# Gate and up products of two of the four shared-expert batches as three fp32r products of parts, in an attention and mixture-of-experts kernel

## The chip, the cores and the metric

The kernel runs on one core of one Trainium2 chip. The metric is the device time of one execution in microseconds (us); lower is better. The core has a matrix engine (TensorE, PE in the profile), a vector engine (VectorE, DVE), an activation engine (ScalarE, ACT), a general engine (GpSimd, POOL) and a queue that only issues transfers (SyncE, SP). All of them read and write the on-chip memory SBUF; PE writes its sums to PSUM, which DVE and ACT read. The engines run by themselves and meet only in semaphores.

## The reference

One transformer block on 4 batches of 512 rows, width 256: a cross attention with 16 heads, then a mixture of 8 experts (2 per row) with a shared expert that every row passes. The change touches the shared expert:

```python
x = x + _L0_xattn_ref(_layernorm(x, axis=-1), ctx_1024, ctx_1024, ...)
x = x + _L0_ffn_ref(_layernorm(x, axis=-1), ...)
# in _L0_ffn_ref, xf is 2048 x 256, HALF = 384
logits = xf @ gate_w.T                      # routing: the two best of 8 experts
for e in range(E):
    g = xf @ wg[e].T
    u = xf @ wu[e].T
    y = jax.nn.silu(g) * u @ w_down[e].T
    out = out + comb[:, e:e + 1] * y
shared = jax.nn.silu(xf @ sg_gate.T) * (xf @ sg_up.T) @ sg_down.T
return (shared + out).reshape(b, t, d)
```

## The kernel before

Each engine has one program, in the order in which its code is written; there is no scheduler. The attention takes the first 262 us. The stretch from there to 318 us does four things at once:

- **Routing**, mainly on DVE: logits, the two best experts of each row, ranks within each expert, and one-hot matrices (`hot_slots`) that PE multiplies into the lists of rows per expert (L957, signal `hot_full`). DVE then writes `token_of` and signals `lists_ready`.
- **The shared expert**, by batch `b` (512 rows) and third `m` of its 384 hidden columns. `shared_up(b)` on PE makes a block of gate and up for each `m`: 4 fp32 matmuls of 128x128 by 512 columns (L910; each is two records in the profile). ACT takes the silu of the gate (`shared_silu`, L1209), DVE multiplies by up (`shared_h`, L1462), and when the three are there, PE multiplies by the down weights (`shared_down`, L920) and DVE adds the result to the rows (`shared_y`, L1484). The blocks alternate between two halves of PSUM, so block n waits for `shared_h` of block n-2.
- **The experts' up weights in two parts.** PE multiplies fp32 numbers in several passes. The kernel avoids it for the experts: a number is the sum of a high part, rounded to the format fp32r, and a low part, the remainder, and a product is the sum of high by high, high by low and low by high. The up weights come in 8 pieces of 128x1536: ACT rounds a piece (`hi_parts`, L1054 into `wup_hi`), DVE subtracts (`lo_part`, L1562 into `wup_lo`). Attention does the same for its projections (L723 to L725).
- **The first tiles of rows.** POOL fetches the rows of the expert tiles by their numbers in `token_of` (L615, indirect transfers, here called gathers). PE transposes a tile (`rows_t`, L969), ACT rounds it, and DVE subtracts (`rows_lo`, L1589), which frees the PSUM bank for the next tile.

Behind `shared_down(2)` PE turns to the experts (L982 to L984). They need all 8 low pieces and take 39 tiles to 475 us. The shared batch 3 and the sums of the experts close the program.

Batches 0, 1 and 2 are the ones before the experts. The change calls batches 1 and 2 "second" and "third". The normalised rows of each batch are stored to DRAM for the gathers (L460 on SP, the last batch at L1213 from ACT).

Of the kernel before, what the change touches and what calls it, by code (L numbers as in the profile page):

```python
# [41 lines left out]
DMA = 16  # L42


def build(nc, x, ctxT, wqT, bq, wkT, bk, wvT, bv, woT, bo, gwT, wupT, wdnT, sgT, suT, sdT, out):
    B, S, D = x.shape
# [5 lines left out]
    C = D // P  # L52
# [27 lines left out]
    with ExitStack() as ctx:  # L80
        def sb(name, shape, dt=F32):
            return ctx.enter_context(nc.sbuf_tensor(name, shape, dt))

        def sem(name):
            return ctx.enter_context(nc.semaphore(name))
# [48 lines left out]
        with nc.sbuf_tensor("e_hT_hi", [P, 2, M, P], F32R) as e_hT_hi, \  # L134
                nc.sbuf_tensor("e_hT_lo", [P, 2, M, P], F32R) as e_hT_lo:
            pass
        moe = sb("moe", [P, MOE])
        e_xT_hi = sb("e_xT_hi", [P, 2, C, P], F32R)
# [74 lines left out]
        lgT = sg[:, M - 1, :]  # L213
        TE = T * E
# [10 lines left out]
        def te():  # L225
# [30 lines left out]
        ld_k, ld_q, ld_ctx, ld_v, ld_o, ld_cv, ld_moe, ld_up = (sem(n) for n in  # L256
            ("ld_k", "ld_q", "ld_ctx", "ld_v", "ld_o", "ld_cv", "ld_moe", "ld_up"))
# [25 lines left out]
        s_up, s_sg, s_h, s_y, s_yfree = (sem(n) for n in ("s_up", "s_sg", "s_h", "s_y", "s_yfree"))  # L283

# [77 lines left out]
        EARLY = 4  # L362

# [10 lines left out]
        def _(sp):  # L374
# [80 lines left out]
            def rows_of(dram, b):  # L455
                return dram[b * S:(b + 1) * S, 0:D].rearrange("(k p) d -> p k d", p=P)

            for b in range(B - 1):
                sp.wait_ge(xs_ready, B + b + 1)
                sp.dma_start(rows_of(xn_d, b), xn2[:, b * QT:(b + 1) * QT, :]).then_inc(xn_stored, DMA)  # L460
# [3 lines left out]
            for c in range(C):  # L464
                sp.dma_start(wup[:, c, :], wupT[c * P:(c + 1) * P]).then_inc(ld_up, DMA)
# [11 lines left out]
        def _(pool):  # L477
# [129 lines left out]

            pool.wait_ge(pad_rows, DMA)
            pool.wait_ge(acc_zeroed, 2 * DMA)
            pool.wait_ge(xn_stored, DMA * B)  # L610
# [27 lines left out]
        def _(pe):  # L638
# [313 lines left out]
            shared_up(1)  # L952
# [8 lines left out]
            shared_up(2, 0, 2)  # L961
# [47 lines left out]
            shared_up(2, 2, 3)  # L1009
# [43 lines left out]
        def _(act):  # L1053
# [144 lines left out]
            def logits_copy(i, cols, src):  # L1198
                act.wait_ge(lt_full, i + 1)
                copy(lgT[:, cols], src).then_inc(lt_read, 1)  # L1200

            ln2_copies(2)
            logits_copy(0, slice(0, S - P), pv_bank[:, 0:S - P])
# [17 lines left out]
            def hi_parts(pieces):  # L1221
                for i in pieces:
                    copy(piece(wup_hi, i), piece(wup, i)).then_inc(up_hi, 1)
# [3 lines left out]
            act.wait_ge(ld_up, DMA * C)  # L1227
            hi_parts(range(0, EARLY))
            for m in range(M):
                shared_silu(1, m)  # L1230
            act.wait_ge(lists_ready, 1)
            act.wait_ge(who_stored, DMA)
            hi_parts(range(EARLY, EARLY + 1))
            shared_silu(2, 0)
            hi_parts(range(EARLY + 1, EARLY + 2))
            shared_silu(2, 1)
            hi_parts(range(EARLY + 2, SPLITS))
# [15 lines left out]
            shared_silu(2, 2)  # L1253
# [33 lines left out]
        def _(dve):  # L1287
# [175 lines left out]

            shared_h(0, 0)
            steps = [0]
# [94 lines left out]
            def lo_part(i):  # L1560
                dve.wait_ge(up_hi, i + 1)
                v.tensor_tensor(piece(wup_lo, i), piece(wup, i), piece(wup_hi, i), ALU.subtract).then_inc(up_lo, 1)  # L1562

            hot_slots(range(0, T))
            shared_y(0)
            hot_slots(range(T, T + T // 2))
            shared_h(1, 0)
            hot_slots(range(T + T // 2, NJ)).then_inc(hot_built, 1)
            shared_h(1, 1)
            lo_part(0)  # L1570
            shared_h(1, 2)
            lo_part(1)
# [5 lines left out]
            v.tensor_scalar(token_of[:], tok, io_np, None, ALU.add).then_inc(lists_ready, 1)  # L1578
            shared_y(1)

            lo_part(2)
            shared_h(2, 0)
            lo_part(3)
            lo_part(EARLY)
            shared_h(2, 1)
# [39 lines left out]
            shared_h(2, 2)  # L1625
            rows_lo(1, 1)
            lo_part(EARLY + 3)
# [91 lines left out]
```

## Time and profile before

| | |
|---|---|
| median of 3 runs | 492.02 us (491.89 to 492.53) |
| the profiled execution | 493.5 us, of it 491.8 us from the first instruction to the last (the span) |
| granted TensorE clock | 0.992 on average |
| busy in the span: PE, DVE, ACT, POOL | 453.9, 314.3, 218.7, 212.6 us |
| start of the experts on PE (L982) | 318.3 us, after the last block of `shared_down(2)` |

In the timeline a matmul's record runs on while the next has started, so the distance of two starts is the time that one costs. "Idle" in brackets is the time that the engine waited before a row, and for whom. Times are from the first instruction. L numbers are lines of the kernel before.

### The profile page before, as it was taken

To read this page: it belongs to the slowest core of one execution; us is meant where nothing else is said; L and a number is where in the kernel's file an instruction comes from. 1 tells how busy PE (TensorE), PEld (TensorE's weight loads), DVE (VectorE), ACT (ScalarE), POOL (GpSimd) and SP (SyncE) were. 2 spreads that over 40 slices of the span, in tenths; PEclk is the share of its full clock that TensorE was granted. 3 is DMA by queue.
4 is the path that set the end of the run, shared out by engine and by line. 5 is a ranking of instruction groups with operands and counts; after the bars stand their busy time and mean duration, and the time that the engine had idled before them with its cause. 6 is when DMAs were issued, how large, how long until landed. Compare 5 with 4: busy or idle time off the path is not lost.

```text
span 491.8 us, 10348 instructions
## 1 busy us (share of the span) xinstructions
PE 453.9 (92%) x3257; PEld 325.3 (66%) x3258; DVE 314.3 (64%) x651; ACT 218.7 (44%) x429; POOL 212.6 (43%) x212
## 2 busy tenths in 40 slices
PE   7879999899999999999978999999999999999993
PEld 5565353664447544564555546699999999999852
DVE  4975767667672856647975895955455545554446
ACT  2257776626573466656863343332232223223210
POOL 4105676743541237302622003036676666665420
PEclk9989999999999999999999999999999999999998
DMA  8592421412224121310398901014444444444379
GB/s 259 106 227 95 130 80 62 155 58 74 69 75 160 34 96 41 117 60 2 104 377 322 327 0 43 1 38 71 74 66 65 74 76 64 66 72 68 36 205 337
DMA packets 45580, 53.93 MB, mean 110 GB/s; under 512 B 7760, under 2 KB 41872, under 8 KB 44912
## 3 DMA queue, kind: packets, MB, share of 16 engines
q1 hardware_dynamic: 34320, 39.77, 25.2%
q0 software_dynamic: 7488, 10.31, 13.1%
q10 hardware_dynamic: 3744, 3.47, 2.7%
q8 instruction: 17, 0.28, 0.2%
q14 instruction: 11, 0.09, 0.1%
HBM read 27.09 MB, written 13.67 MB: 83 GB/s over the span
## 4 chain that ended last, share of the span: by engine, by line
PE 63%; DVE 18%; ACT 6%; DMA 5%; issue 4%; SPq 1%; DVEq 0%; ACTq 0%; POOLq 0%
PE set_a L659 7%; PE set_a L983 6%; PE set_a L984 6%; PE set_a L982 6%; PE set_b L689 6%; DVE attention L1379 4%; ACT attention L1133 4%; PE set_b L679 3%; PE set_b L1001 3%; PE set_a L890 3%; PE set_b L1002 3%; PE set_b L1003 3%; PE set_b L992 2%; PE set_a L701 2%; PE set_a L910 2%
## 5 line engine op out<-in xcount | busy, mean ns | idle before, releaser
L1379 DVE TENSOR_REDUCE attention<-set_a 128x2 f32<-128x1024 f32 (+2 forms) x96 | 95.9, 1040 | 26.4 <-PE set_a L661 24.4
L1133 ACT ACTIVATE attention<-set_b 128x512 f32<-128x512 f32 (+1 forms) x176 | 87.9, 569 | 49.4 <-PE set_b L679 36.1
L543 POOL TENSOR_SCALAR_AFFINE_SELECT attention<-attention 128x512 f32<-128x512 f32 x64 | 42.8, 683 | 89.7 <-ACT attention L1133 89.7
L623 POOL DMA_INDIRECT sum_rows<-moe,token_of x39 | 61.8, 1586 | 43.8 <-issue 29.5
L659 PE MATMUL set_a<-attention 96*128 96x512 bf16 (+3 forms) x256 | 61.5, 305 | 5.1 <-DVE attention L1379 4.8
L615 POOL DMA_INDIRECT e_x<-normed_rows,token_of x39 | 39.5, 1013 | 61.3 <-DVE token_of L1578 34.9
L1246 ACT ACTIVATE moe<-set_a 128x384 f32<-128x384 f32 x39 | 19.2, 492 | 105.0 <-PE set_a L984 105.0
L679 PE MATMUL set_b<-attention 99*128 99x512 bf16 (+3 forms) x256 | 58.9, 303 | 7.0 <-ACT attention L1133 5.3
L1603 DVE TENSOR_TENSOR moe<-set_a,moe 128x384 f32<-128x384 f32 x39 | 21.7, 558 | 62.8 <-ACT moe L1246 34.5
L659 PEld LDWEIGHTS set_a<-attention 96*128 96x128 bf16 x256 | 25.4, 99 | 44.9 <-DVE attention L1379 17.4
L982 PE MATMUL set_a<-wup_hi,e_xT_hi 128*128 x156 | 53.1, 340 | 0.0
L983 PE MATMUL set_a<-wup_lo,e_xT_hi 128*128 x156 | 52.9, 339 | 0.0
L984 PE MATMUL set_a<-wup_hi,e_xT_lo 128*128 x156 | 52.8, 338 | 0.0
L661 PE MATMUL set_a<-maskb,identb 128*128 128x128 bf16 x256 | 49.6, 222 | 0.0
L689 PE MATMUL set_b<-attention 128*32 128x128 f32 (+3 forms) x512 | 43.8, 441 | 1.3 <-POOL attention L543 1.2
L1001 PE MATMUL set_b<-w_down_hi,e_hT_hi 128*128 x117 | 36.4, 311 | 1.3 <-DVE moe L1615 0.8
L679 PEld LDWEIGHTS set_b<-attention 99*128 99x128 bf16 x256 | 19.2, 97 | 27.5 <-ACT attention L1133 18.2
L1054 ACT ACTIVATE attention<-set_b 12x512 bf16<-12x512 f32 (+4 forms) x48 | 26.0, 595 | 20.3 <-PE set_b L647 11.2
L524 POOL TENSOR_TENSOR attention<-attention 128x512 f32<-128x512 f32 x14 | 15.9, 1157 | 42.8 <-ACT attention L1054 21.4
L1003 PE MATMUL set_b<-w_down_hi,e_hT_lo 128*128 x117 | 32.9, 281 | 0.0
L1002 PE MATMUL set_b<-w_down_lo,e_hT_hi 128*128 x117 | 32.8, 281 | 0.0
L1054 ACT ACTIVATE attention<-attention 128x512 bf16<-128x512 f32 x32 | 19.2, 643 | 26.7 <-DVE attention L1327 21.2
(179 smaller groups left out, 893.7 us busy)
## 6 DMA issues: line engine op xcount, KB each, us to landing
attention<-attention SPq DMA_DIRECT2D x182, 64.0 KB, 2.6
wup<-in_wupT SPq DMA_DIRECT2D x2, 3072.0 KB, 14.6
sum_rows<-attention SPq DMA_DIRECT2D x2, 2048.0 KB, 13.5
wup<-sum_rows SPq DMA_DIRECT2D x8, 512.0 KB, 6.9
attention<-in_ctxT SPq DMA_DIRECT2D x7, 512.0 KB, 6.5
w_down<-in_wdnT SPq DMA_DIRECT2D x3, 1024.0 KB, 5.1
x_res<-in_x SPq DMA_DIRECT2D x4, 512.0 KB, 7.5
out<-x_res ACTq DMA_DIRECT2D x8, 256.0 KB, 4.0
```

Of the source, the lines that this page charges most:

```text
L623: g.indirect_dma_start(acc[i], bass.IndirectOffsetOnAxis(token_of[:, t:t + 1], 0), e_y[:, t % 2, :], None, compute_op=ALU.add).then_inc(ad ...
L659: mm(dst, qstack[0:ROWS, g // 2, h, k * P:w], kstack[0:ROWS, g // 2, h, 0:w], start=True, stop=False)
L661: last = mm(dst[:, k * P:w], identb[:], maskb[:], start=False, stop=True)
L679: last = mm(bank(par)[:, i * w:(i + 1) * w], kstack[0:ROWS + 3, g // 2, h, k * P:(k + 1) * P], qstack[0:ROWS + 3, g // 2, h, k * P:S], sta ...
L689: last = mm(pv_bank[32 * h:32 * h + 32, k * P:S], vaug[:, k, HG * g + h, :], pT[k][:, h, :], start=k == 0, stop=k == QT - 1, tile_position ...
L982: mm(dst, e_xT_hi[:, a, c, :], wup_hi[:, c, cols], start=c == 0, stop=False)
L983: mm(dst, e_xT_hi[:, a, c, :], wup_lo[:, c, cols], start=False, stop=False)
L984: last = mm(dst, e_xT_lo[:, a, c, :], wup_hi[:, c, cols], start=False, stop=c == C - 1)
L1001: mm(dst, e_hT_hi[:, a, m, :], wdn_hi[:, m, cols], start=m == 0, stop=False)
L1003: last = mm(dst, e_hT_lo[:, a, m, :], wdn_hi[:, m, cols], start=False, stop=m == M - 1)
L1133: nc.scalar.activation(pT[k][:, h:h + heads, :], bank(par)[:, 0:heads * (S - k * P)], ACT.Exp).then_inc(b_free, 1)
L1379: v.tensor_reduce(dst, src, AX.X, ALU.max, negate=True).then_inc(a_free, 1)
```

## The change

Batches 1 and 2 of the shared expert's gate and up are no longer made by fp32 matmuls but by `shared_up_parts`: 12 fp32r matmuls a block in place of 4 fp32 ones. For that ACT rounds the shared weights (2 copies of 128x768) and the rows of the two batches (2 of 128x1024), and DVE subtracts as often. The parts lie in the place of rows whose store to DRAM must be over first, so the store semaphore is split in three. `shared_up(2)` was cut in two with a `rows_t` between; now it is one piece. Pieces 0 and the last of the experts' weights get their low part on POOL (`up_low`), the other six on DVE. The high parts start when the first half of the weights has landed.

```diff
+        w_hi = moe_r[:, 0:2 * C * HALF].rearrange("p (a c n) -> p a c n", a=2, c=C)
+        w_lo = moe_r[:, 2 * C * HALF:4 * C * HALF].rearrange("p (a c n) -> p a c n", a=2, c=C)
+        x_hi = {1: second_hi[:], 2: moe_r[:, (B - 1) * QT * D:B * QT * D].rearrange("p (c n) -> p c n", c=C)}
...
+        PIECES = [0, 1, 2, 3, 6, 7, 4, 5]
...
+            def up_low(i):
+                pool.wait_ge(up_hi, i + 1)
+                w = PIECES[i]
+                g.tensor_tensor(piece(wup_lo, w), piece(wup, w), piece(wup_hi, w), ALU.subtract).then_inc(up_lo, 1)
+
+            pool.wait_ge(hot_built, 1)
+            up_low(0)
...
             for t in range(NX):
                 rows_in_tile(t)
+            up_low(SPLITS - 1)
...
+            def shared_up_parts(b, lo=0, hi=M):
+                pe.wait_ge(sw_lo, 2)
+                pe.wait_ge(sx_lo, b)
+                for m in range(lo, hi):
+                    n = b * M + m
+                    pe.wait_ge(s_h, n - 1)
+                    for a, dst in enumerate(gu[n % 2]):
+                        for c in range(C):
+                            high, low = w_hi[:, a, c, m * P:(m + 1) * P], w_lo[:, a, c, m * P:(m + 1) * P]
+                            mm(dst, high, x_hi[b][:, c, :], start=c == 0, stop=False)
+                            mm(dst, high, x_lo[b][:, c, :], start=False, stop=False)
+                            last = mm(dst, low, x_hi[b][:, c, :], start=False, stop=c == C - 1)
+                    last.then_inc(s_up, 1)
...
-            shared_up(1)
+            shared_up_parts(1)
...
-            shared_up(2, 0, 2)
+            shared_up_parts(2)
...
-            shared_up(2, 2, 3)
...
             ln2_copies(2)
+            act.wait_ge(xn_first, DMA * 2)
+            act.wait_ge(ld_moe, DMA * 4)
+            copy(w_hi[:, 1], wsu[:]).then_inc(sw_hi, 1)
+            copy(w_hi[:, 0], wsg[:]).then_inc(sw_hi, 1)
+            rows_hi(1)
...
             shared_h(0, 0)
+            dve.wait_ge(sw_hi, 2)
+            dve.wait_ge(xn_third, DMA)
+            for a, w in enumerate((wsg, wsu)):
+                v.tensor_tensor(w_lo[:, a], w[:], w_hi[:, a], ALU.subtract).then_inc(sw_lo, 1)
+            rows_low(1)
```

On DVE, from the second half of the lists to the low part of the second tile of rows, the program before had these rows (`wup_lo` is a `lo_part`, `moe<-set_a,moe` a `shared_h`, `x_res` a `shared_y`, `e_xT_lo` a `rows_lo`):

```order
L1578 TENSOR_SCALAR token_of<-router 128x39 [waits hot_read]
L1484 TENSOR_TENSOR x_res<-set_b,x_res 128x1024 [waits s_y]
L1562 TENSOR_TENSOR wup_lo<-wup,wup_hi 128x1536 [waits up_hi]
L1462 TENSOR_TENSOR moe<-set_a,moe 128x512 [waits s_sg]
L1562 TENSOR_TENSOR wup_lo<-wup,wup_hi 128x1536 [waits up_hi] x2
L1462 TENSOR_TENSOR moe<-set_a,moe 128x512 [waits s_sg]
L1562 TENSOR_TENSOR wup_lo<-wup,wup_hi 128x1536 [waits up_hi]
L1589 TENSOR_TENSOR e_xT_lo<-set_b,e_xT_hi 128x256 [waits e_xhi]
L1562 TENSOR_TENSOR wup_lo<-wup,wup_hi 128x1536 [waits up_hi]
L1462 TENSOR_TENSOR moe<-set_a,moe 128x512 [waits s_sg]
L1589 TENSOR_TENSOR e_xT_lo<-set_b,e_xT_hi 128x256 [waits e_xhi]
L1562 TENSOR_TENSOR wup_lo<-wup,wup_hi 128x1536 [waits up_hi]
```

The changed program has these in the same stretch:

```order
L1638 TENSOR_SCALAR token_of<-router 128x39 [waits hot_read]
L1623 TENSOR_TENSOR wup_lo<-wup,wup_hi 128x1536 [waits up_hi]
L1544 TENSOR_TENSOR x_res<-set_b,x_res 128x1024 [waits s_y]
L1623 TENSOR_TENSOR wup_lo<-wup,wup_hi 128x1536 [waits up_hi]
L1513 TENSOR_TENSOR moe<-set_a,moe 128x512 [waits s_sg]
L1623 TENSOR_TENSOR wup_lo<-wup,wup_hi 128x1536 [waits up_hi]
L1513 TENSOR_TENSOR moe<-set_a,moe 128x512 [waits s_sg]
L1623 TENSOR_TENSOR wup_lo<-wup,wup_hi 128x1536 [waits up_hi]
L1513 TENSOR_TENSOR moe<-set_a,moe 128x512 [waits s_sg]
L1623 TENSOR_TENSOR wup_lo<-wup,wup_hi 128x1536 [waits up_hi]
L1650 TENSOR_TENSOR e_xT_lo<-set_b,e_xT_hi 128x256 [waits e_xhi]
L1623 TENSOR_TENSOR wup_lo<-wup,wup_hi 128x1536 [waits up_hi]
```

The third `shared_h` of batch 2 moved ahead of the first `rows_lo`; behind that `shared_h` stands one `lo_part`, then the `rows_lo`.

On POOL, from the last constant of the routing on, the changed program reads as follows. Before, both `wup_lo` rows were absent and the rest was the same, with one store semaphore.

```order
L612 IOTA router 128x1 x2
L625 TENSOR_TENSOR wup_lo<-wup,wup_hi 128x1536 [waits up_hi,hot_built]
L638 DMA e_x<-normed_rows,token_of 128x260 [waits xn_stored,xn_third,who_stored,xn_first,lists_ready,acc_zeroed,pad_rows]
L638 DMA e_x<-normed_rows,token_of 128x260 x3
L625 TENSOR_TENSOR wup_lo<-wup,wup_hi 128x1536 [waits up_hi]
L638 DMA e_x<-normed_rows,token_of 128x260 [waits e_wr] x3
```

One subtraction stands ahead of the four first gathers, the other behind them.

## Rows read from the trace of the kernel before

**Rows 1.** The page's part 4: the chain that ended last, by engine
```profile
PE 63%; DVE 18%; ACT 6%; DMA 5%; issue 4%; SPq 1%; DVEq 0%; ACTq 0%; POOLq 0%
```
**Rows 2.** The same chain in order of time, 286 to 319: start us, us
```profile
286.11 2.61 DVE router L1557 x16
...
291.80 3.70 PE set_a L910 x8
295.50 1.18 PE set_b L957 x32
296.67 5.26 PE set_b L920 x24
301.93 6.88 PE set_a L910 x16
...
309.43 2.74 ACT wup_hi L1054 x2
...
312.48 0.44 DVE e_xT_lo L1589
313.05 0.41 PE set_b L969 x2
...
318.64 0.18 PE set_a L982
```
**Rows 3.** Timeline of PE: the third and the twelfth matmul of an attention fp32r block
```profile
70.21 0.39 PE L725 MATMUL set_a<-w_down_hi,w_down_lo 128*128 128x512 f32 x1
...
72.30 0.40 PE L725 MATMUL set_a<-w_down_hi,w_down_lo 128*128 128x512 f32 x1
```
**Rows 4.** Timeline of DVE in the stretch of the shared expert
```profile
267.03 0.69 DVE L1462 TENSOR_TENSOR moe<-set_a,moe 128x512 f32<-128x512 f32 x1 [0.32 <-ACT moe L1209]
270.01 0.29 DVE L1478 COPY router<-set_a 128x128 f32<-128x128 f32 x1 [2.29 <-PE set_a L817]
...
306.64 3.42 DVE L1562 TENSOR_TENSOR wup_lo<-wup,wup_hi 128x1536 fp32r<-128x1536 f32 x2
```
**Rows 5.** Timelines of POOL and DVE where both subtract or add in SBUF
```profile
236.11 1.22 DVE L1401 TENSOR_TENSOR w_down_lo<-w_down,w_down_hi 128x1024 fp32r<-128x1024 f32 x1
...
242.07 3.33 POOL L512 TENSOR_TENSOR x_res<-x_res,attention 128x1024 f32<-128x1024 f32 x1
243.10 3.39 DVE L1401 TENSOR_TENSOR w_down_lo<-w_down,w_down_hi 128x1024 fp32r<-128x1024 f32 x1
...
98.65 2.37 POOL L554 TENSOR_TENSOR attention_parts<-attention,w_down_hi 128x1024 fp32r<-128x1024 f32 x1
100.04 1.22 DVE L1358 TENSOR_TENSOR attention<-set_a,attention 128x1024 f32<-128x1024 f32 x1 [3.70 <-PE set_a L701]
```
**Rows 6.** Timeline of POOL and DVE: gathers, and the subtraction beside the last
```profile
302.63 0.96 POOL L615 DMA_INDIRECT e_x<-normed_rows,token_of  x1 [0.30 <-issue]
303.89 1.80 POOL L615 DMA_INDIRECT e_x<-normed_rows,token_of  x1 [0.30 <-issue]
303.11 1.75 DVE L1562 TENSOR_TENSOR wup_lo<-wup,wup_hi 128x1536 fp32r<-128x1536 f32 x1
```
**Rows 7.** The store of batch 1's rows (L460), and ACT's timeline around it
```profile
L460 SPq DMA_DIRECT2D normed_rows<-moe x1: 1503/1503/1503, 254.0 to 254.0; - x1
...
DMA to landing us min/median/max: 7.4/7.4/7.4
264.89 0.21 ACT L1059 ACTIVATE std<-st_a 128x4 f32<-128x4 f32 x1 [1.82 <-DVE st_a L1307]
```
**Rows 8.** Windows of PE: stretch, us, PE busy (x), granted clock, DMA share, GB/s
```profile
26.60:29.90 3.30, 1.27 (x11) 1.00 1.17 135
30.00:33.30 3.30, 3.30 (x23) 0.50 1.02 325
...
484.00:487.30 3.30, 0.00 (x0) 1.00 1.09 367
487.40:490.70 3.30, 0.00 (x0) 0.50 1.09 384
```

More of the change, by code:

```diff
@@ L136, in build @@
             pass
+        with nc.sbuf_tensor("moe_parts", [P, MOE], F32R) as moe_r:
+            pass
         moe = sb("moe", [P, MOE])
+        with nc.sbuf_tensor("second_rows_hi", [P, C, S], F32R) as second_hi:
+            pass
         e_xT_hi = sb("e_xT_hi", [P, 2, C, P], F32R)
@@ L213, in build @@
         lgT = sg[:, M - 1, :]
+        w_hi = moe_r[:, 0:2 * C * HALF].rearrange("p (a c n) -> p a c n", a=2, c=C)
+        w_lo = moe_r[:, 2 * C * HALF:4 * C * HALF].rearrange("p (a c n) -> p a c n", a=2, c=C)
+        x_hi = {1: second_hi[:], 2: moe_r[:, (B - 1) * QT * D:B * QT * D].rearrange("p (c n) -> p c n", c=C)}
+        xT_parts = moe_r[:, T * D:T * D + C * N].rearrange("p (c n) -> p c n", c=C)
+        x_lo = {b: xT_parts[:, :, b * S:(b + 1) * S] for b in (1, 2)}
         TE = T * E
@@ L255, in build @@
         ld_x = [sem(f"ld_x{b}") for b in range(B)]
-        ld_k, ld_q, ld_ctx, ld_v, ld_o, ld_cv, ld_moe, ld_up = (sem(n) for n in
-            ("ld_k", "ld_q", "ld_ctx", "ld_v", "ld_o", "ld_cv", "ld_moe", "ld_up"))
+        ld_k, ld_q, ld_ctx, ld_v, ld_o, ld_cv, ld_moe = (sem(n) for n in
+            ("ld_k", "ld_q", "ld_ctx", "ld_v", "ld_o", "ld_cv", "ld_moe"))
+        ld_up = [sem(f"ld_up{c}") for c in range(C)]
         consts, pads, fills, pad_rows = sem("consts"), sem("pads"), sem("fills"), sem("pad_rows")
@@ L283, in build @@
         s_up, s_sg, s_h, s_y, s_yfree = (sem(n) for n in ("s_up", "s_sg", "s_h", "s_y", "s_yfree"))
+        sw_hi, sw_lo, sx_hi, sx_lo = (sem(n) for n in ("sw_hi", "sw_lo", "sx_hi", "sx_lo"))
+        xn_first, xn_third = sem("xn_first"), sem("xn_third")
         e_in = [sem(f"e_in{i}") for i in range(NX)]
@@ L459, in _ @@
                 sp.wait_ge(xs_ready, B + b + 1)
-                sp.dma_start(rows_of(xn_d, b), xn2[:, b * QT:(b + 1) * QT, :]).then_inc(xn_stored, DMA)
+                sp.dma_start(rows_of(xn_d, b), xn2[:, b * QT:(b + 1) * QT, :]
+                             ).then_inc(xn_first if b < 2 else xn_third, DMA)
             sp.wait_ge(a_free, A_ALL)
@@ L464, in _ @@
             for c in range(C):
-                sp.dma_start(wup[:, c, :], wupT[c * P:(c + 1) * P]).then_inc(ld_up, DMA)
+                sp.dma_start(wup[:, c, :], wupT[c * P:(c + 1) * P]).then_inc(ld_up[c], DMA)
             sp.wait_ge(who_ready, TOP_K)
@@ L605, in _ @@
             count(io_np, [[0, 1]], N, 1)
+            def up_low(i):
[4 more added lines that the diff above has]
+            up_low(0)
             pool.wait_ge(pad_rows, DMA)
             pool.wait_ge(acc_zeroed, 2 * DMA)
-            pool.wait_ge(xn_stored, DMA * B)
+            pool.wait_ge(xn_first, DMA * 2)
+            pool.wait_ge(xn_third, DMA)
+            pool.wait_ge(xn_stored, DMA)
             pool.wait_ge(who_stored, DMA)
@@ L1200, in logits_copy, with rows_hi @@
                 copy(lgT[:, cols], src).then_inc(lt_read, 1)
+            def rows_hi(b):
+                copy(x_hi[b], xn2T[:, :, b * S:(b + 1) * S]).then_inc(sx_hi, 1)
             ln2_copies(2)
+            act.wait_ge(xn_first, DMA * 2)
[3 more added lines that the diff above has]
+            rows_hi(1)
             logits_copy(0, slice(0, S - P), pv_bank[:, 0:S - P])
@@ L1220, in _, with hi_part @@
             nc.scalar.activation(ex, dl, ACT.Exp).then_inc(ex_ready, 1)
-            def hi_parts(pieces):
-                for i in pieces:
-                    copy(piece(wup_hi, i), piece(wup, i)).then_inc(up_hi, 1)
+            def hi_part(i):
+                copy(piece(wup_hi, PIECES[i]), piece(wup, PIECES[i])).then_inc(up_hi, 1)
             for m in range(1, M):
                 shared_silu(0, m)
[L1227 to L1230, printed above, removed]
+            act.wait_ge(ld_up[0], DMA)
+            for i in range(EARLY):
+                hi_part(i)
+            shared_silu(1, 0)
+            act.wait_ge(xn_stored, DMA)
+            rows_hi(2)
+            shared_silu(1, 1)
+            shared_silu(1, 2)
+            act.wait_ge(ld_up[1], DMA)
+            act.wait_ge(hot_full, 1)
+            hi_part(EARLY)
+            hi_part(EARLY + 1)
             act.wait_ge(lists_ready, 1)
             act.wait_ge(who_stored, DMA)
-            hi_parts(range(EARLY, EARLY + 1))
+            hi_part(EARLY + 2)
             shared_silu(2, 0)
-            hi_parts(range(EARLY + 1, EARLY + 2))
+            hi_part(EARLY + 3)
             shared_silu(2, 1)
-            hi_parts(range(EARLY + 2, SPLITS))
+            shared_silu(2, 2)
             def rows_t(t, a):
@@ L1252, in _ @@
             rows_t(0, 0)
-            shared_silu(2, 2)
             rows_t(1, 1)
@@ L1462, in shared_h, with rows_low @@
                 v.tensor_tensor(sg[:, m, :], up_, sg[:, m, :], ALU.mult).then_inc(s_h, 1)
+            def rows_low(b):
+                dve.wait_ge(sx_hi, b)
+                v.tensor_tensor(x_lo[b], xn2T[:, :, b * S:(b + 1) * S], x_hi[b], ALU.subtract).then_inc(sx_lo, 1)
             shared_h(0, 0)
+            dve.wait_ge(sw_hi, 2)
[3 more added lines that the diff above has]
+            rows_low(1)
             steps = [0]
@@ L1561, in lo_part @@
                 dve.wait_ge(up_hi, i + 1)
-                v.tensor_tensor(piece(wup_lo, i), piece(wup, i), piece(wup_hi, i), ALU.subtract).then_inc(up_lo, 1)
-            hot_slots(range(0, T))
+                w = PIECES[i]
+                v.tensor_tensor(piece(wup_lo, w), piece(wup, w), piece(wup_hi, w), ALU.subtract).then_inc(up_lo, 1)
+            hot_slots(range(0, T // 2))
             shared_y(0)
-            hot_slots(range(T, T + T // 2))
+            hot_slots(range(T // 2, T))
             shared_h(1, 0)
-            hot_slots(range(T + T // 2, NJ)).then_inc(hot_built, 1)
+            hot_slots(range(T, NJ)).then_inc(hot_built, 1)
             shared_h(1, 1)
-            lo_part(0)
+            rows_low(2)
             shared_h(1, 2)
-            lo_part(1)
             dve.wait_ge(hot_full, 1)
@@ L1578, in _ @@
             v.tensor_scalar(token_of[:], tok, io_np, None, ALU.add).then_inc(lists_ready, 1)
+            lo_part(1)
             shared_y(1)
@@ L1583, in _ @@
             lo_part(3)
+            shared_h(2, 1)
             lo_part(EARLY)
-            shared_h(2, 1)
+            shared_h(2, 2)
             def rows_lo(t, a):
@@ L1624, in _ @@
             lo_part(EARLY + 2)
-            shared_h(2, 2)
             rows_lo(1, 1)
-            lo_part(EARLY + 3)
             weights(0, 0, True)
```

## The prediction

> **What bounds the kernel now.** I read the chain that ended last first. By engine it is 63% PE [rows 1]. In order of time [rows 2] it shows what orders the stretch that the change touches: PE multiplies the lists (295.50), runs `shared_down(1)` (296.67 to 301.93) and two fp32 blocks of `shared_up(2)` (6.88 us, so 3.44 a block). Then the chain leaves PE. From 309.43 ACT rounds two weight pieces, DVE makes the low part of the first tile (`rows_lo`, 312.48), and only then PE may transpose the second tile (313.05), run `shared_down(2)` and start the experts (318.3 for the first of them, 318.64 on the chain). From there on PE's tiles follow each other to the end and nothing in them changes. So the whole effect is how far the experts' start moves, and that start hangs on two things: when PE has finished the blocks, and when the first `rows_lo` is done. Call the latter R; it starts at 312.48 now. From R the experts start 5.8 us later, whatever came before.
>
> **What PE gains.** In the attention, 9 steps of the same fp32r form (128x128 by 512) take 72.30 - 70.21 = 2.09 us [rows 3], so 0.232 each and 12 x 0.232 = 2.79 a block. Six blocks save 6 x (3.44 - 2.79) = 3.9 us.
>
> **What the parts cost at the front.** ACT's four copies at first: it waits for the store of batch 1, issued at 254.0 and landed 7.4 later, at 261.4 [rows 7]. A copy of 1536 columns takes 1.37 [rows 2], so 768, 768 and 1024 take some 2.4, and a copy of logits 0.5: done by 264.4. ACT's next work is wanted at 264.89, for which it idled 1.82 before [rows 7]. Hidden with half a us to spare.
>
> DVE's three subtractions stand between `shared_h(0, 0)` and the router. DVE is free at 267.03 + 0.6 and idles 2.29 until 270.01 [rows 4]. Two back-to-back subtractions of 1536 take 3.42 [rows 4], of which 0.08 is the tail of the last record: 1.67 each. By columns 768 takes 0.87, and 1024 takes 1.13 (its full record is 1.22 [rows 5]). Sum 2.87, end 270.5: **0.5 us late**. All of the router stands behind it and DVE has no other gap before the lists' matrices are built, so that 0.5 is paid in full. The third block of batch 1 starts at 291.8 now [rows 2]; it waits for a `shared_h` that DVE reaches behind 24 one-hot matrices. 16 of these take 2.61 [rows 2]; 8 of them move behind that `shared_h`, which comes 1.3 - 0.5 = 0.8 earlier for it. The block runs from 291.0 to 293.9, the lists at 293.9 (1.6 earlier than the 295.50 of now), `shared_down(1)` from 295.1. The matrices, 0.5 late, are complete at 293.5.
>
> **What follows on DVE.** POOL's first piece starts when the matrices are built, at 293.5. Its price: POOL takes 2.37 for 1024 [rows 5], so about 3.5 for 1536. Does it slow DVE? When POOL added in SBUF at 242.07, DVE's subtraction of 1024, issued at 243.10, took 3.39 where 1.22 is usual: it ended 1.1 after POOL's end at 245.40. It stood still until POOL was done. POOL itself took 3.33 instead of 2.37, because the DVE subtraction before it had to end first. But a DVE operation with one input in PSUM took its usual 1.22 beside POOL's subtraction at 98.65 [rows 5]. So `lo_part` and the new `rows_low` exclude POOL's pieces, `shared_h`, `shared_y` and `rows_lo` do not. (By the Trainium skill, "SBUF — State Buffer", Who interferes with whom, it is the same: two SBUF inputs on VectorE and a GpSimd instruction that reads SBUF block each other for the whole instruction.)
>
> `rows_low(2)` on DVE is wanted at 294.1 and gets in at 297.0, ends 298.2; `shared_h(1, 2)` ends 298.8, so the last third of `shared_down(1)` starts 0.35 late; `token_of` is written at 299.3 (0.4 later than now). `shared_down(1)` ends at 300.7, and three blocks of 2.79 end at 303.5, 306.3 and **309.1**. Now the third ends at 312.3 (301.93 + 6.88, one transposed tile, 3.44). PE is 3.2 us ahead there.
>
> DVE, paced by these blocks (a silu and a `shared_h` behind each; a `shared_h` takes 0.6 to the next start, its record 0.69 [rows 4], and I take as much for the silu): `shared_h(2, 0)` at 304.3, `lo_part` 304.9 to 306.6, `shared_h(2, 1)` at 307.1, `lo_part` 307.7 to 309.4, `shared_h(2, 2)` 309.9 to 310.5, `lo_part` 310.5 to 312.2, then R. So even with nothing in the way R stands at 312.2, 0.3 before today's 312.48. **The gain of PE ends in a new wait**: PE idles from 309.3 to 312.8, because R stands behind `shared_h(2, 2)` and a `lo_part`.
>
> **POOL's second piece** of 3.5 us must now find its place. It is ready when the four gathers are issued. Two gathers free of a DVE subtraction follow each other after 1.26 [rows 6]. The fourth took 1.80 instead of 0.96; a `lo_part` begun at 303.11 held SBUF until 304.8, 0.9 before that gather's end [rows 6]. I take it that a gather also waits for a subtraction that it meets. The new lists are followed by a `lo_part` at once, so the first gather waits to 301.0 and ends at 302.0, the second meets the next one (302.1 to 303.8) and ends at 304.7, the third meets or just passes that of 304.9, the fourth that of 307.7. POOL is then ready between 308 and 310.4. Whoever asks first gets SBUF, and DVE's `lo_part` ahead of R asks at 310.5:
> - Ready before 309.4: the piece runs 309.4 to 312.9, the `lo_part` ends at 314.6. R is 2.1 later than today.
> - Ready at 310.4: 310.4 to 313.9, `lo_part` to 315.6. R is 3.1 later.
>
> I take 2.5.
>
> **The clock.** PE would idle 5 to 6 us. The rows show what idleness does: after 3.3 us with PE busy 1.27 the granted clock fell to 0.50, the lower of its levels of 1.2 and 2.4 GHz, and stayed there for 3.3 us at least although PE was busy throughout; after 3.3 us without a matmul at the end it fell too [rows 8]. A fall costs half of the time that it lies over work: 0 to 1.7 for one such stretch. `shared_down(2)` and the first experts stand there. I add 1.3.
>
> **Sum.** 2.5 + 1.3 = 3.8 us on the profiled execution's 493.5. The median of the runs is 1.5 lower, so 492.0 + 3.8 = **495.8**. This case reaches from 2.1 + 0.5 to 3.1 + 1.7: 494.6 to 496.8.
>
> **Rivals.**
> - *Gathers are free of the lock* (the fourth's 1.80 is one row, and its cause may be another). Then they are issued by 305.3 and POOL's piece takes SBUF when the `lo_part` ends at 306.6, to 310.1. DVE's next, wanted at 307.7, ends at 311.8, `shared_h(2, 2)` at 312.4, the `lo_part` at 314.1: R 1.6 later; with a clock cost of 1.2, 494.8. The Trainium skill, "SBUF — State Buffer", Who interferes with whom, leans to it: it infers that a two-input subtraction does not hold up descriptor writing. Chance 0.15.
> - *DVE asks first at 310.5*, by 0.1 or 0.2 us. POOL's piece then starts at 312.2 beside `rows_lo`, which it does not disturb; the last `lo_part` ends at 317.4, in time. R at 312.2. PE still idles 3.5 us. If the clock falls: -0.3 and 0.7 to 1.7, so 492.4 to 493.4; if it stays: 491.7. Chance 0.2, three quarters of it with the fall.
> - *Faster.* It takes that DVE's three subtractions fit in the free 2.37 us (0.72 ns a column, against 1.09 measured), which gives back the 0.5, and that POOL's pieces do not stop DVE, which gives back 0.35 on `shared_down(1)`. Then PE is done at 308.2, R at 311.3, 1.2 earlier: 490.8. It decides at the router's first copy: before 270.1 or not. Against it stand [rows 4, 5]. Were R not behind the `lo_part` at all, all of 3.9 less 0.5 would come through (488.6), but the order of DVE excludes it. Chance 0.1.
> - *The store lands late*: each tenth beyond 261.9 moves the last normalisation and all behind it by as much. It comes on top of any case, hence 0.4 more at the top.
>
> **How the numbers follow.** The forecast's own case has 0.55. Range for 8 in 10: 491.4 (below the quiet form of the second rival) to 497.2. A measurement of this kernel tells 0.2%, 1.0 us, from no change. Faster by more than that: 0.1 and a little for what I overlook, 0.12. Within: the second rival without the fall and the half of it with the fall that stays under 1.0, and some more, 0.2. Slower: 0.68.
>
> **What would show it.** Blocks of L947 to L949 at 2.8 us; the router's copy at 270.5; the lists' matmul at 293.9; `rows_low(2)` on DVE at over 3 us; PE idle 3.5 to 7 us ahead of the second `rows_t`; the last POOL subtraction ending before DVE's fifth `lo_part`, which shows over 3 us; a stretch of clock 0.50 near 313 to 318; no difference inside the experts' loop. Wrong it would be if POOL's second piece lies beside PSUM work only, if the clock stays at 1.00 through a gap of 3.5 us or more, or if the experts' loop itself changes its pace.

## The result, and the profile after

The changed kernel takes 498.55 us (median of 6 executions, 497.3 to 500.64) against 492.0 us of the kernel before in the same comparison (6 executions, 491.63 to 492.57): the ratio is 1.0123, 95% interval 1.0104 to 1.0143. It is slower, as forecast, but by 6.5 us (6.0 by the ratio) instead of 3.8, and the median is outside the range. In its profiled execution (497.8 us) the span is 496.1 us and the mean granted clock 0.984.

Before the stretch of the change begins, this execution is 1.3 us ahead of the one of before. ACT's timeline shows it at `std` (264.89 in [rows 7]), and also shows the new copies in front of it. (Columns in all timelines: start, us, engine, line, operation, what it writes and reads, number; in brackets the idle time before the row and whom it waited for.)

```profile
260.79 0.84 ACT L1091 ACTIVATE moe_parts<-w_su 128x768 fp32r<-128x768 f32 x1 [3.85 <-DMA normed_rows<-moe]
261.54 0.83 ACT L1091 ACTIVATE moe_parts<-w_sg 128x768 fp32r<-128x768 f32 x1
262.27 1.04 ACT L1091 ACTIVATE second_rows_hi<-moe 128x1024 fp32r<-128x1024 f32 x1
...
263.59 0.19 ACT L1096 ACTIVATE std<-st_a 128x4 f32<-128x4 f32 x1
```

The lead arises in the first 42 us, among instructions that the change doesn't touch (a load of `x_res` on which DVE waits 1.17 us instead of 2.27, and a shorter wait for PE near 31 us), so 1.3 us are added to each difference below. Rounding lies in ACT's idle time, as forecast. Next, DVE of the changed kernel, ahead of the router and at the end of the stretch:

```profile
266.33 0.95 DVE L1523 TENSOR_TENSOR moe_parts<-w_sg,moe_parts 128x768 fp32r<-128x768 f32 x1
267.19 0.95 DVE L1523 TENSOR_TENSOR moe_parts<-w_su,moe_parts 128x768 fp32r<-128x768 f32 x1
268.06 1.22 DVE L1517 TENSOR_TENSOR moe_parts<-moe,second_rows_hi 128x1024 fp32r<-128x1024 f32 x1
269.20 0.28 DVE L1538 COPY router<-set_a 128x128 f32<-128x128 f32 x1
...
292.74 4.12 DVE L1517 TENSOR_TENSOR moe_parts<-moe,moe_parts 128x1024 fp32r<-128x1024 f32 x1
...
309.00 4.93 DVE L1623 TENSOR_TENSOR wup_lo<-wup,wup_hi 128x1536 fp32r<-128x1536 f32 x1
313.85 0.41 DVE L1650 TENSOR_TENSOR e_xT_lo<-set_b,e_xT_hi 128x256 fp32r<-128x256 f32 x1
```

The router's first copy is at 269.20 against 270.01 [rows 4], with the lead 0.5 late. Two subtractions took 4.12 and 4.93 us where 1.22 and 1.75 are usual. R (the first `rows_lo`, L1650 here) is at 313.85 against 312.48 [rows 2], with the lead 2.7 late. POOL's timeline shows what they met, its two pieces and, between them, four gathers that take 1.75 to 2.54 where two of before took 0.96 and 1.80 [rows 6]:

```profile
292.32 3.47 POOL L625 TENSOR_TENSOR wup_lo<-wup,wup_hi 128x1536 fp32r<-128x1536 f32 x1 [28.67 <-DVE router L1617]
298.82 1.75 POOL L638 DMA_INDIRECT e_x<-normed_rows,token_of  x1 [3.04 <-DVE token_of L1638]
300.88 2.41 POOL L638 DMA_INDIRECT e_x<-normed_rows,token_of  x1 [0.31 <-issue]
303.60 2.54 POOL L638 DMA_INDIRECT e_x<-normed_rows,token_of  x1 [0.30 <-issue]
306.44 2.41 POOL L638 DMA_INDIRECT e_x<-normed_rows,token_of  x1 [0.30 <-issue]
308.88 3.42 POOL L625 TENSOR_TENSOR wup_lo<-wup,wup_hi 128x1536 fp32r<-128x1536 f32 x1
```

The second piece began 0.12 us ahead of DVE's low part. The chain in order of time (start, us, what) and the windows of PE (stretch, us, PE busy, granted clock, DMA share, GB/s) show what followed on PE:

```profile
308.39 0.69 DVE moe L1513
309.08 4.84 DVE wup_lo L1623
313.93 0.34 DVE e_xT_lo L1650
...
314.41 0.66 PE set_b L1007 x2
315.06 7.59 PE set_b L958 x24
322.66 0.18 PE set_a L1020
```
```profile
306.00:309.00 3.00, 1.94 (x10) 1.00 0.16 44
309.00:312.90 3.90, 0.00 (x0) 1.00 0.11 34
313.00:316.30 3.30, 1.89 (x6) 0.50 0.00 0
316.40:319.80 3.40, 3.40 (x9) 0.50 0.14 39
319.90:323.00 3.10, 3.10 (x16) 1.00 0.15 43
```

PE was done with the blocks and the first transposes at about 308, idled 6.5 us until 314.41, and then made `shared_down(2)` largely at the lower level of 1.2 GHz: 7.59 us, where the chain of before has 5.18:

```profile
313.46 5.18 PE set_b L920 x24
```

The experts start on the chain at 322.66 instead of 318.64, with the lead 5.3 us late. The rest to 5.6 (4.3 of span and 1.3 of lead) comes behind.

### The profile page after: what moved, and what is told of

It is laid out like the page before. It is cut to its first block, busy times and chain, and to the rows that moved or that the text cites. A ratio compares the mean times of both kernels' runs of the same rounds, so it can differ in the third digit from the quotient of the medians.

```text
span 496.1 us, 10411 instructions
## 1 busy us (share of the span) xinstructions
PE 454.3 (92%) x3281; PEld 333.0 (67%) x3282; DVE 321.0 (65%) x653; ACT 222.1 (45%) x433; POOL 223.4 (45%) x214
## 4 chain that ended last, share of the span: by engine, by line
PE 62%; DVE 17%; ACT 7%; DMA 6%; issue 4%; SPq 3%; ACTq 0%; POOL 0%; DVEq 0%; POOLq 0%
PE set_a L683 6%; PE set_a L1021 6%; PE set_a L1020 6%; PE set_a L1022 6%; PE set_b L713 5%; ACT attention L1170 4%; PE set_b L1039 3%; PE set_b L703 3%; DVE attention L1430 3%; PE set_a L725 3%; PE set_b L1040 3%; PE set_b L1041 3%; PE set_b L1030 2%; PE set_a L914 2%; DVE w_down_lo L1452 2%
## 5 line engine op out<-in xcount | busy, mean ns | idle before, releaser
L638 POOL DMA_INDIRECT e_x<-normed_rows,token_of x39 | 43.6, 1119 | 26.8 <-DVE weight_of L1660 12.8
```

## Experiments

Each kernel was compared with the kernel before on the same chip; that one's medians there were 492.79 (beside the second piece on DVE, first `rows_lo` first, `shared_down(2)` first and 16 filling matmuls), 492.75 (beside both pieces on DVE, POOL's pieces alone, 8 filling and all on DVE, new order) and 492.84 (beside the other four), while in the comparison above it was 492.0. Single executions of one kernel lie up to 5.4 us apart here, the longer ones mostly at a lower mean granted clock. The ratios are not the quotients of the medians, so a difference is given by both where they disagree. The table gives for each profiled execution two distances of DVE rows: from the copy that opens the router to the first `hidden` of the experts (in before 270.01 to 321.33), and from there to the last row of DVE, the second of two at L1680 before and L1739 after. Neither contains the differences of the first 265 us or the router's 0.5. In four of the profiled executions (first `rows_lo` first, 16 filling, 8 filling, 16 tiny) the clock also fell right behind the router's first copy, for 3.4 us somewhere between 269.3 and 273.6; there the way from that copy to the lists takes 29.3 to 29.4 us instead of the 28.2 of the changed kernel, so 1.1 to 1.2 of the first column is that fall's.

| kernel | median us (executions) | ratio to before, 95% interval | router to `hidden` | `hidden` to end |
|---|---|---|---|---|
| before | 492.0 (6) | | 51.3 | 166.6 |
| changed | 498.55 (6) | 1.0123 [1.0104, 1.0143] | 56.1 | 166.9 |
| changed, again | 500.66 (5) | 1.0155 [1.0134, 1.0177] | 56.0 | 166.9 |
| second piece on DVE | 493.78 (12) | 1.0035 [1.0016, 1.0054] | 50.3 | 166.7 |
| both pieces on DVE | 493.27 (12) | 1.0029 [1.0010, 1.0049] | 49.9 | 166.9 |
| POOL's pieces alone | 495.40 (9) | 1.0047 [1.0031, 1.0063] | 53.3 | 166.7 |
| first `rows_lo` first | 492.17 (12) | 0.9995 [0.9975, 1.0016] | 50.6 | 166.8 |
| `shared_down(2)` first | 495.52 (12) | 1.0036 [1.0013, 1.0058] | 52.4 | 167.8 |
| 16 filling matmuls | 498.88 (5) | 1.0129 [1.0109, 1.0149] | 54.8 | 169.4 |
| 8 filling matmuls | 498.37 (4) | 1.0111 [1.0092, 1.0129] | 54.9 | 169.2 |
| 16 tiny matmuls | 501.37 (5) | 1.0177 [1.0156, 1.0198] | 57.5 | 169.4 |
| all on DVE, new order | **489.06** (6) | 0.9933 [0.9910, 0.9956] | 46.6 | 166.8 |
| before in that order | 491.65 (12) | 0.9975 [0.9958, 0.9993] | 50.5 | 166.4 |
| new order, second piece on POOL | 491.25 (12) | 0.9971 [0.9957, 0.9985] | 48.6 | 167.0 |

**Theory:** POOL's second piece held up the low part ahead of R, and PE's idle time behind R let the clock fall. **Rivals:** the loss sits in the router's delay, the gathers or the first piece; or the clock fell, or `shared_down(2)` was slow, for another reason.

### POOL's pieces

The second piece goes back to DVE:

```diff
                 rows_in_tile(t)
-            up_low(SPLITS - 1)
...
             rows_lo(1, 1)
+            lo_part(SPLITS - 1)
```

> The changed kernel with POOL's second low part given back to DVE, behind the second rows_lo; POOL keeps the first. Lock theory (POOL's 3.42 us subtraction L625 at 308.88 held DVE's low part from 309.00 to 313.93, and with it the first rows_lo, R): the low part takes 1.75, R comes at 310.8 instead of 313.85, TensorE's shared_down(2) is done about 317.2 instead of 322.3 (3.1 from R, about 2 to 2.6 if the clock stays up): 493.4 to 495.5 us, against 498.6 of the changed kernel. Rival (the loss sits elsewhere, in the router's delay, the gathers or the first POOL piece, and DVE's added work takes back what it frees): R moves by under 1 us and the time is 497.6 or more.

DVE's timeline in that kernel:

```profile
309.66 1.75 DVE L1622 TENSOR_TENSOR wup_lo<-wup,wup_hi 128x1536 fp32r<-128x1536 f32 x1
311.33 0.42 DVE L1649 TENSOR_TENSOR e_xT_lo<-set_b,e_xT_hi 128x256 fp32r<-128x256 f32 x1
```

The low part takes 1.75 again and the median is 493.78, as the theory gave. With more work on DVE the kernel is 4.3 us (by the ratios, 1.0123 and 1.0035, intervals apart) to 4.8 us (by the medians) faster than the changed one. Its profile, of the shortest of the twelve executions, shows no lower clock from 308 to 323, though PE idled 3.28 us ahead of the second transposes; five of the twelve took 494.5 to 496.96 at a mean clock of 0.981 to 0.987, so the clock may have fallen in those. Then the first piece too:

```diff
-            pool.wait_ge(hot_built, 1)
-            up_low(0)
...
+            lo_part(0)
             lo_part(1)
             shared_y(1)
```

> The changed kernel with both of POOL's low parts on DVE (the first just before lo_part(1), the second behind the second rows_lo), so that POOL makes none; the fp32r blocks and their parts stay. Lock theory: rows_low(2), held for 2.9 us by POOL's first piece, takes 1.22, the last third of shared_down(1) isn't late (0.35 us), DVE is 2.9 - 1.75 = 1.15 us ahead of the kernel with only the second piece moved, and the end is bound by TensorE's blocks, 0.35 us earlier than there: 493.2 to 493.8 us against 493.8. Rival (the first piece cost as much as the second, about 3 us of the end): 491 us or less. Second rival (DVE is now the bound and wants POOL's help): 494.5 us or more.

493.27: inside the forecast, and too near the 493.78 to be told from it. Moving the first piece, though it had held `rows_low(2)` for 2.9 us, gained at most a few tenths; there PE had work in hand. The pieces alone, in the kernel before:

```diff
+            pool.wait_ge(hot_built, 1)
+            up_low(0)
             pool.wait_ge(pad_rows, DMA)
...
                 rows_in_tile(t)
+            up_low(SPLITS - 1)
...
-            lo_part(0)
...
-            lo_part(EARLY + 3)
```

> The kernel before with the other half of the change alone: POOL makes the first and the last of the eight low parts, at the same two places of its queue (behind hot_built, behind the fourth gather), DVE no longer makes them; the blocks stay fp32. Lock theory: the last piece waits for ACT's copy and starts at about 312.2, just ahead of DVE's low part at 312.82, which is held until about 317.3 and holds shared_h(2,2); the last third of shared_down(2) is late by about 1 us, the first piece costs nothing at the end: 493 to 495 us. The piece alone doesn't reach R, which goes at 312.48, so the price is far under the 3 us that it had in the changed kernel. Rival (POOL's pieces cost the same wherever the blocks stand): 495.5 us or more; rival (off DVE, they gain): 492.2 us or less.

POOL's timeline of that kernel, and DVE's:

```profile
313.88 3.44 POOL L610 TENSOR_TENSOR wup_lo<-wup,wup_hi 128x1536 fp32r<-128x1536 f32 x1 [6.57 <-ACT wup_hi L1061]
```
```profile
314.10 0.42 DVE L1595 TENSOR_TENSOR e_xT_lo<-set_b,e_xT_hi 128x256 fp32r<-128x256 f32 x1 [0.16 <-ACT e_xT_hi L1061]
314.44 4.49 DVE L1569 TENSOR_TENSOR wup_lo<-wup,wup_hi 128x1536 fp32r<-128x1536 f32 x1
318.85 0.68 DVE L1469 TENSOR_TENSOR moe<-set_a,moe 128x512 f32<-128x512 f32 x1
```

The piece stopped the low part behind R and, with it, `shared_h(2, 2)`, just as expected; PE waited 1.05 us for that `shared_h` ahead of the last third of `shared_down(2)`, which is the 1 that I gave, but the stretch is 2.0 us longer than before's (53.3 against 51.3). Of the rest, 0.41 is a wait put down to "issue" ahead of the experts, and 0.5 isn't explained. The median of 495.40 is at the rival's edge of 495.5 and above my range, so the price was too low and only the place was right. POOL's help alone makes the old kernel slower. `rows_lo`, which reads PSUM, took its usual 0.42 beside the piece.

### The order behind the blocks

```diff
-            lo_part(EARLY + 1)
             rows_lo(0, 0)
+            lo_part(EARLY + 1)
```

> The changed kernel with one statement moved on DVE: the first rows_lo ahead of the low part lo_part(5) that stood before it; both POOL pieces stay. Lock and order theory (R was ready to go at 309.1, since ACT's copy of its rows ended at 308.63, and waited only behind a held low part): R at 309.1 to 309.5, TensorE's idle stretch falls from about 6 to under 2 us, shared_down(2) runs 310.2 to 315.4 at the full clock, and the first expert waits for the last low part at about 316 instead of 322.3: 491.5 to 493.5 us. Rival (TensorE's lateness is not set by R but by what follows, the low parts or the gathers): 496.5 us or more.

With both of POOL's pieces in place this gives 492.17, 6.4 us off the changed kernel (6.3 by the ratios). DVE's timeline shows the same collision, now behind R:

```profile
310.22 0.41 DVE L1650 TENSOR_TENSOR e_xT_lo<-set_b,e_xT_hi 128x256 fp32r<-128x256 f32 x1
310.55 6.28 DVE L1623 TENSOR_TENSOR wup_lo<-wup,wup_hi 128x1536 fp32r<-128x1536 f32 x2
```

PE's matmul groups of the same kernel (busy us, mean ns, idle before) have `shared_down(2)` at full speed and only 0.6 us of waiting for the last low part:

```profile
L958 PE MATMUL set_b<-w_sd,moe 128*128 128x256 f32 x24 | 5.3, 379 | 0.0
L1020 PE MATMUL set_a<-wup_hi,e_xT_hi 128*128 x2 | 0.8, 390 | 0.6 <-DVE wup_lo L1623 0.6
```

So the lock as such costs little; the lock in front of R cost the time. The other way to fill the idle time leaves DVE alone and moves PE's work:

```diff
+            shared_down(2)
             rows_t(1, 1, 1, 1)
-            shared_down(2)
```

> The changed kernel with shared_down(2) moved ahead of the second transposes of rows on TensorE; everything else stays, POOL's pieces too. If the loss is only that TensorE stood behind R with work at hand (shared_down(2) needs nothing of R, its last input is there at 309.1), it runs 309.1 to 314.3 in the idle stretch at the full clock, and the first expert waits for the last low part at 315.95 instead of 322.3: 491.5 to 493.5 us. Rival (the low parts and DVE's queue bound the start of the experts, not TensorE): no more than 2 us gained, 496.5 us or more.

The median, 495.52, is between the two forecasts. `shared_down(2)` did run in the gap (308.64, 5.34 us), but PE then waited again, in PE's timeline and windows:

```profile
315.28 0.41 PE L1007 MATMUL set_b<-ident,e_x 128*128 128x128 f32 x2 [1.29 <-DVE e_xT_lo L1650]
317.71 0.68 PE L1020 MATMUL set_a<-wup_hi,e_xT_hi 128*128 x1 [2.02 <-DVE e_xT_lo L1650]
```
```profile
314.00:316.70 2.70, 0.41 (x2) 1.00 0.00 0
316.90:320.20 3.30, 2.49 (x8) 0.50 0.11 23
```

Three of the twelve executions took 491.83 to 493.20 us with a mean clock of 0.993 to 0.995, the other nine 494.37 to 497.11 with 0.985 to 0.988. I had priced the move without a fall, and those three are where I put it. The profiled one, in which PE waited 3.3 us and then fell to the lower clock, is of the nine. That the three kept it is read from their means alone. In the profiled one the lower level held from 316.9 to 323.7, which reaches 1.2 us beyond the first `hidden` and is part of its 167.8 in the last column.

### The clock by itself

```diff
             rows_t(0, 0, 0, 1, True)
+            for i in range(16):
+                mm(Bk[:, 1, :], w_hi[:, 0, 0, 0:P], x_hi[2][:, 0, :], start=True, stop=True)
             rows_t(1, 1, 1, 1)
```

> The changed kernel with 16 matmuls of 128x512 in fp32r put in TensorE's idle stretch, between the first and the second transposes of rows; their result is read by nobody. They last 16 x 0.23 = 3.7 us and end at 311.7, before R at 313.85, so they delay nothing. Clock theory (the half clock from 312.99 to 319.82 follows from TensorE standing idle from 307.9 to 314.4, and costs 2.6 us on shared_down(2)): the granted clock stays 1.00 there, shared_down(2) takes 5.2 instead of 7.6 us, 495.5 to 496.5 us. Rival (the clock falls for another reason, or shared_down(2) is slow for another reason, such as its reads): no change, 497.5 to 499.5 us.

The PE rows of this kernel:

```profile
308.74 3.90 PE L1048 MATMUL set_b<-moe_parts 128*128 128x512 f32 x16
315.51 0.41 PE L1007 MATMUL set_b<-ident,e_x 128*128 128x128 f32 x2 [2.87 <-DVE e_xT_lo L1652]
315.75 5.35 PE L958 MATMUL set_b<-w_sd,moe 128*128 128x256 f32 x24
```

The clock stayed at 1.00 and `shared_down(2)` took 5.35, yet the median, 498.88, is what the rival gave. The table shows why: the last column grew by 2.5 us. Something behind the start of the experts took the gain back. Two controls, the first with 8 fp32 matmuls of 128x512 (`wsg` by `xn2T`) in place of the 16:

> The kernel with filling matmuls again, with 8 fp32 matmuls of 128x512 in place of the 16 in fp32r: 8 x 0.43 = 3.4 us of work in the same idle stretch with half as many instructions. As before the clock should stay at 1.00 over shared_down(2) and the first expert start 2.6 us earlier, counted from the block starts. It asks where the 2.8 us went that the kernel with 16 lost again inside the experts' loop and behind it: if they hang on where the loop lies in TensorE's program, the loss comes out another size here and the time may reach 496 us; if they hang on the earlier start of the experts (a collision with transfers or with POOL), the loss is again 2.5 to 3 us and the time 498.5 to 499.5 us.

Half as many instructions, about as much more in the last column (2.3 us) and about the same time: the number isn't what matters, and I couldn't tell yet whether their presence or the kept clock did. The second control leaves 16 instructions at the place, with 8 columns each:

> A control for the two kernels with filling matmuls: 16 matmuls at the same place, but only 8 columns wide, so that TensorE has as many more instructions and still stands idle for nearly as long. If added instructions by themselves cost the 2.5 us that those kernels lost again in and behind the experts' loop, both losses are there now (half clock over shared_down(2), and the loop's): 500.5 to 501.5 us. If the loop's loss came with the kept clock or the earlier start, this one equals the changed kernel: 498 to 499 us.

501.37: both losses at once. PE idles 4.79 us before the second transposes:

```profile
308.47 1.93 PE L1048 MATMUL set_b<-moe_parts 128*128 128x8 f32 x16
315.19 0.66 PE L1007 MATMUL set_b<-ident,e_x 128*128 128x128 f32 x2 [4.79 <-DVE e_xT_lo L1652]
```

Now the three kernels with added matmuls can be compared among themselves. The one whose clock fell takes 57.5 us from router to `hidden`, the two whose clock stayed take 54.8 and 54.9: **the fall costs 2.6 to 2.7 us**, and 2.5 to 3.0 by the medians. The other 2.3 to 2.5 us, in the last column, belong to added instructions as such, whatever the clock did.

The changed kernel once more, for its other executions:

> The changed kernel once more, for more executions of it beside the others, with the mean granted clock of each. Clock theory: after an idle stretch of more than 6 us every execution falls to the half clock over shared_down(2) (means near 0.984), and none lies near 495.5 us, where the kept clock would put it; the median is again 498 to 499 us.

Of five executions two took 498.19 and 499.09 at a mean clock of 0.984, and three 500.66 to 501.37 at 0.980 to 0.981. None was near 495.5, as expected; the median is 1.7 above the range I gave, and the three long ones have the lower mean clock. Where that was can't be seen, as only the execution of 498.19 has a trace. In that trace all that matters comes again: POOL's second piece starts 0.12 us ahead of DVE's low part (309.35 and 309.47), that one takes 4.93, PE idles 6.46, and the clock is low from 313.3 to 320.1.

### A faster kernel

All low parts on DVE, each a place earlier from the fourth on; the first `rows_lo` straight behind `shared_h(2, 2)`; `shared_down(2)` ahead of the second transposes, as above. Of this the edit of DVE's queue is shown:

```diff
             lo_part(2)
-            shared_h(2, 0)
             lo_part(3)
-            shared_h(2, 1)
+            shared_h(2, 0)
             lo_part(EARLY)
+            shared_h(2, 1)
+            lo_part(EARLY + 1)
             shared_h(2, 2)
...
-            lo_part(EARLY + 1)
             rows_lo(0, 0)
             lo_part(EARLY + 2)
+            lo_part(SPLITS - 1)
             rows_lo(1, 1)
```

> All that the runs so far point to, on top of the changed kernel: all eight low parts on DVE, each from the fourth on one place earlier in its queue (into the waits for the blocks of the third batch), the first rows_lo straight behind shared_h(2,2), and on TensorE shared_down(2) ahead of the second transposes of rows. Counted from the kernel with rows_lo first (blocks done 309.0, first expert 317.0, 492.17 us): shared_down(2) 308.9 to 314.2, second transposes 314.6, DVE's last low part done by 314.5, first expert at 314.9 to 315.0, so 2.0 to 2.1 us off: 489.9 to 490.4 us, faster than both kernels by 0.4% or more. Rival (the start of the experts doesn't carry through to the end, as in the kernel with 16 filling matmuls): 491.5 us or more.

489.06 us, 0.4 to 0.9% faster than the kernel before, and 0.8 below my range. The chain in order of time shows no other engine between the blocks and the experts:

```profile
307.00 0.23 PE set_a L946
307.24 0.22 PE set_b L1004 x2
307.45 5.18 PE set_b L955 x24
...
312.85 0.18 PE set_a L1017
```

What of it is due to the fp32r blocks, and what to the order? The kernel before with the same order:

> The kernel before with the order of the fastest kernel so far and nothing else of it: the fp32 blocks stay, DVE makes all eight low parts, from the fourth on one place earlier, the first rows_lo follows shared_h(2,2), TensorE runs all three blocks of the third batch, then the first transposes, shared_down(2), the second transposes. TensorE has no idle stretch to fill there (blocks done at 312.3 already): shared_down(2) 312.3 to 317.6, first expert at 318.0 instead of 318.64: 491.9 to 492.7 us. So the fp32r blocks would be worth about 3 us in the fastest kernel (489.06). Rival (the order alone made that kernel fast, the fp32r blocks give nothing): 489.5 us or less.

491.65, 0.25 below the range. So the order is worth 1.2 us by itself (0.9975, interval 0.9958 to 0.9993). The fp32r blocks, with all that the change brings along for them, are worth another 2.1 (by the ratios) to 2.6 (by the medians), of the 3.9 less 0.5 that PE and the router left. In the table the stretch is 3.9 shorter (50.5 to 46.6); the router's 0.5 and 0.4 behind the first `hidden` come off that, and a further 0.4 to 0.9 isn't accounted for. Last, POOL's second piece in the faster kernel:

> The fastest kernel so far (489.06 us; first expert at 312.6 in its profile) with POOL's second piece put back behind its fourth gather. The gathers end at 302.7 there and ACT's copy for the piece at 303.7, so POOL has the port from about 303.9 to 307.3 and holds the low part at 304.06 until 309.0. Lock theory: everything behind it on DVE is 3.2 us late, less the one low part that DVE no longer makes at the end: shared_h(2,2) 312.1 instead of 308.7 (the last third of shared_down(2) 1.2 late), last low part 314.3, first expert 314.3 to 314.6: 1.7 to 2.0 us slower, 490.7 to 491.1 us. Rival (with slack ahead of R the lock costs nothing): 489.4 us or less.

491.25, slower by 1.9 (ratios) to 2.2 (medians), where I gave 1.7 to 2.0, and 0.15 above the range. POOL started at 303.40, 0.26 ahead of DVE, which then took 4.87:

```profile
303.66 4.87 DVE L1621 TENSOR_TENSOR wup_lo<-wup,wup_hi 128x1536 fp32r<-128x1536 f32 x1
```

## Why the prediction was wrong

- **PE's blocks.** Right: 0.227 to 0.233 us a step. Of the 3.4 us left by the forecast's own sum, 2.1 to 2.6 came through in the faster kernel, once nothing stood in the way.
- **ACT and the router.** Right: hidden copies, 0.5 us late at the router's copy.
- **The first piece.** Right: `rows_low(2)` took 4.12 us and the effect at the end was small.
- **A new wait behind R.** Right: PE idled from about 308 to 314.41.
- **The second piece.** The case "ready at 310.4" came true, with POOL 0.12 us ahead (in both traces of this kernel). (By the Trainium skill, "SBUF — State Buffer", Who interferes with whom, issue order decides who blocks; POOL's leads of 0.12 and, in the last experiment, 0.26 us agree.) R was 2.7 late where the forecast took 2.5. That gathers wait for subtractions that they meet held in all four. The rival without it didn't come: by the same section of the Trainium skill a subtraction would not hold up the writing of descriptors, but here gathers that met one took 1.75 to 2.54 us.
- **The clock. This is the step that failed**, in size: "0 to 1.7 for one such stretch", of which 1.3 was taken. The lower level held for 6.8 us, 313.0 to 319.8, and most of it lay over `shared_down(2)`. It cost 2.6 to 2.7 us by the control. Its price was read from a stretch of 3.3 us [rows 8] and that length was taken as the most. There the clock was indeed back behind it:

```profile
33.50:36.70 3.20, 2.48 (x30) 1.00 0.88 290
```

  But PE had been busy throughout that stretch. Here it stood idle for the first 1.4 us of the low clock, and the low clock held for twice as long. The forecast had no row of such a case and no reason to carry the shorter length over. Behind R the experts' start grew by 2.65 us (8.81 against 6.16), which agrees with the control; R itself is 2.7 late. With 2.65 in place of 1.3 the sum would be 497.15, just inside the range. The other 1.4 are R's 0.2 and the rest, below.
- **The rest.** The table shows 0.3 of the 5.6 behind the first `hidden`. From 5.6 us in the profiled pair to 6.5 in the medians, 0.9 remains (0.4 by the ratio). It is open: of the other five executions two had a lower mean clock than the profiled one (0.980 and 0.983), but two at the same 0.984 were longer as well, 498.52 and 499.81.
- **"DVE asks first"**, the rival at 0.2, was missed by 0.12 us. With its clock at the forecast's price it gave 493.4 at most, so it was luck of a tenth of a us which of two cases 2.4 us apart came.
- **"Faster".** Its condition is mis-reckoned: 2.37 us for the 2560 columns of the three subtractions are 0.93 ns a column and not 0.72. They took 2.87 us, 1.12 ns a column, so it makes no difference to the case. Its remark that with R free of the low part 3.4 us would come through (488.6) is half right: with the first `rows_lo` first the loss went (492.17), but hardly any gain came: PE still waited 1.61 us for R and 0.61 for the last low part there. It took the whole new order, without POOL's pieces, to reach 489.06.

## What to carry to other kernels

When work on one engine gets shorter, read what the next wait stands behind in the other engines' queues, and move that short operation ahead of long ones before measuring the gain: here one moved statement was worth 6.4 us. Don't give POOL a long SBUF-only operation where DVE makes such operations on PE's way: it cost about 2 us or more in three kernels, and well under 1 us only where PE had work in hand. And price an idle stretch of PE at more than itself: here 2.6 us of slow clock came on top.

## What the runs showed of the hardware

- Added matmuls cost time far behind their place. In PE's groups from 325 us to 484 us, the matmuls that open the experts' down product idle 1.2 us in the changed kernel, 2.1 in the one with 16 filling matmuls and 2.4 in the one with 16 tiny ones, where 1.0 and 1.4 us are put down to "issue", a wait for nothing that the profile shows:

```profile
L1039 PE MATMUL set_b<-w_down_hi,e_hT_hi 128*128 x117 | 36.4, 311 | 1.2 <-DVE moe L1676 0.8
```
```profile
L1039 PE MATMUL set_b<-w_down_hi,e_hT_hi 128*128 x117 | 36.4, 311 | 2.4 <-issue 1.4 <-DVE moe L1678 0.9
```

  By DVE's `hidden` rows of the 39 tiles, 1.0 to 1.1 us of it gather inside the loop, in steps of at most 0.3 us at about every fourth turn, and 1.2 to 1.5 lie behind the loop; the second trace of the changed kernel stays within 0.2 us of the first. 8 and 16 instructions cost about the same. Why, no run here shows.
- An operation held up by the other engine's lock ended 1.6 us after it (POOL until 312.30, DVE until 313.93), nearly its whole 1.75, as if little or nothing of it had been done before.
- The low clock held for two lengths. Behind the router's copy, with PE at work throughout, it was 3.4 us (270.1 to 273.5, 16 filling matmuls). With PE idle at the start of it, it was 6.8 us: in both traces of the changed kernel, with `shared_down(2)` first and with 16 tiny matmuls.
